# Regrouping the small products of the second attention layer, with a changed set-up, a changed step between the layers and both last norms on VectorE

## The reference

```
def layer0(x, emb, mask):                       # 16 heads of 32
    xn = layernorm(x) * norm_w + norm_b
    q, k, v = xn @ q_w + q_b, xn @ k_w + k_b, (xn @ v_w + v_b) * mask
    att = softmax over keys of (q k^T per head, masked)
    y = att @ v
    scale, shift = split(silu(emb) @ emb_w + emb_b)
    h = layernorm(y) * sb_w + sb_b;  h = h * (1 + scale) + shift
    return x + silu(h) @ out_w + out_b

def layer1(x, emb, mask):                       # 8 heads of 64
    xn = layernorm(x) * ln_w + ln_b
    q = softmax over a head's features of (xn @ Wq + bq)
    k = softmax over tokens of (xn @ Wk + bk, masked)
    v = (xn @ Wv + bv) * mask
    y = q @ (k^T v)                             # per head
    (the same norm of y, scale, shift, silu, output product, + x)
```

## Time and profile before

| | |
|---|---|
| median of 3 runs | 1053.91 us (1051.83 to 1054.78) |
| the profiled execution's own time | 1052.0 us |
| its span | 1048.6 us |
| TensorE busy | 1022.5 us, 98% of the span |
| VectorE, ScalarE, GpSimd busy | 772.7, 610.6, 588.1 us |
| mean granted TensorE clock | 0.997 of full |

### The profile page before, as it was taken

How to read it: one execution, slowest core, us unless ns; L and a number is a source line. 1 busy time by engine, 2 the same in 40 slices (tenths; PEclk the granted TensorE clock), 3 DMA queues, 4 the chain that set the end, 5 groups by cost and what they waited for, 6 DMA issues and landing times. The chain is left out here.

```text
span 1048.6 us, 26047 instructions
## 1 busy us (share of the span) xinstructions
PE 1022.5 (98%) x8558; PEld 890.0 (85%) x8558; DVE 772.7 (74%) x1347; ACT 610.6 (58%) x2021; POOL 588.1 (56%) x871
## 2 busy tenths in 40 slices
PE   7899999999999999999997999999999999999997
PEld 6679888988889888898886888888888888888885
DVE  6656766677666766678679787878778877778886
ACT  6358676876768766776777454434434444443353
POOL 3455456555465456554577465666556555566632
PEclk9999999999999999999999999999999999999999
DMA  9752111211212111120113211222211112112101
GB/s 302 246 184 67 39 52 43 64 55 35 60 44 65 47 40 53 55 65 34 56 51 116 81 63 50 67 67 65 65 65 56 39 55 65 55 55 65 45 31 50
DMA packets 46117, 73.72 MB, mean 70 GB/s; under 512 B 8274, under 2 KB 14546, under 8 KB 46068
## 3 DMA queue, kind: packets, MB, share of 16 engines
q1 hardware_dynamic: 46066, 73.11, 21.8%
q10 hardware_dynamic: 2, 0.00, 0.0%
HBM read 56.28 MB, written 16.81 MB: 70 GB/s over the span
## 5 line engine op out<-in xcount | busy, mean ns | idle before, releaser
L683 ACT ACTIVATE prob<-prob,neg_max 128x128 f32<-128x128 f32 x512 | 198.6, 395 | 77.7 <-DVE neg_max L983 77.7
L483 POOL TENSOR_SCALAR stat<-stat 128x1 f32<-128x1 f32 x128 | 34.7, 271 | 321.7 <-DVE stat L945 295.3
L1363 PE MATMUL bank<-xt_hi,w_hi 128*128 128x256 f32 x752 | 213.8, 284 | 0.0
L1364 PE MATMUL bank<-xt_lo,w_hi 128*128 128x256 f32 x752 | 209.4, 279 | 0.0
L1365 PE MATMUL bank<-xt_hi,w_lo 128*128 128x256 f32 x752 | 209.4, 278 | 0.0
L1363 PE MATMUL bank<-w_hi,xt_hi 128*128 128x512 f32 x384 | 157.6, 410 | 0.0
L1365 PE MATMUL bank<-w_hi,xt_lo 128*128 128x512 f32 x384 | 151.2, 394 | 0.0
L1364 PE MATMUL bank<-w_lo,xt_hi 128*128 128x512 f32 x384 | 150.4, 392 | 0.0
L1364 PEld LDWEIGHTS bank<-xt_lo,w_hi 128*128 128x128 f32 x752 | 141.9, 189 | 1.3
L1363 PEld LDWEIGHTS bank<-xt_hi,w_hi 128*128 128x128 f32 x752 | 141.6, 188 | 1.5 <-DVE z_a L1027 0.2
L1365 PEld LDWEIGHTS bank<-xt_hi,w_lo 128*128 128x128 f32 x752 | 141.7, 188 | 0.0
(11 more groups left out here) (130 smaller groups left out, 2347.4 us busy)
## 6 DMA issues: line engine op xcount, KB each, us to landing
x_in<-in_x_dram SPq DMA_DIRECT2D x32, 256.0 KB, 2.7
x_res<-in_x_dram SPq DMA_DIRECT2D x32, 256.0 KB, 2.6
between_layers<-x_res SPq DMA_DIRECT2D x32, 256.0 KB, 2.0
x_in<-between_layers SPq DMA_DIRECT2D x32, 256.0 KB, 3.3
x_res<-between_layers SPq DMA_DIRECT2D x28, 256.0 KB, 2.6
out_dram<-x_res SPq DMA_DIRECT2D x28, 256.0 KB, 2.0
room<-in_L_cond_W_emb_dram SPq DMA_DIRECT2D x8, 512.0 KB, 6.6
prob<-in_L_cond_emb_w_dram SPq DMA_DIRECT2D x4, 512.0 KB, 11.2
```

What stands on the lines that cost most here:

```text
L483: pool.tensor_scalar(v[:, 8:9], v[:, 7:8], EPS, None, ALU.add).then_inc(s[a_in].sem, 1)
L683: last = act.activation(prob[:, b, i, :], prob[:, b, i, :], ACT.Exp, bias=neg_max[:, b, i:i + 1], accum_out=row_sum[:, b, h:h + 1])
L1363: pe.matmul(o, a_hi, b_hi, start=start, stop=False)
L1364: pe.matmul(o, a_hi, b_lo, start=False, stop=False)
```

## The change

Seven things change together. (1) TensorE's order in `step1` and the first part of `drain`: both `turn_k`, both `keys`, both `keys_values`, both outputs, both `query`, both `values` and both `turn_yn` now stand together, and PSUM banks are dealt anew. (2) In `step1`, the scale (`film1`), `tanh`, `silu`, high and low part of both sequences of pair `k` move from the end of their step to the beginning of the next, where that pair is `late`. (3) POOL's second `v_mask` stands before the two residuals. (4) In `step_mixed` POOL makes `norm2` before the residuals and `v_mask`. (5) At the start VectorE norms both first pairs, with POOL making only their factors, and one values product comes earlier on TensorE. (6) `keep_busy` adds seven products of `ident` with itself, whose result nobody reads, around the first `turn`s. (7) In `drain` both last norms end on VectorE.

```diff
-        SECOND = dict(X=(0, 1), K=(6, 7), V=(0, 6), Q=(2, 4), KT=(2, 4), QT=(3, 3), KV=(4, 4), Y=(5, 1), H=(3, 7), O=(5, 1))
+        SECOND = dict(X=(0, 1), K=(6, 0), V=(6, 0), Q=(2, 4), KT=(2, 4), QT=(5, 5), KV=(4, 2), Y=(5, 4), H=(3, 7), O=(1, 3))
-        DRAIN = SECOND | dict(V=(0, 3), Q=(2, 4), KT=(6, 7), QT=(2, 4), KV=(0, 3), Y=(6, 7), H=(0, 3), O=(5, 4))
+        DRAIN = SECOND | dict(V=(7, 6), Q=(2, 3), KT=(0, 4), QT=(2, 2), KV=(6, 7), Y=(0, 4), H=(6, 7), O=(5, 3))
...
-                for b in range(GROUP):
-                    rsqrt(b, 0, "aggr", "rstd_a", "rstd_b", "neg_mean", pair(0) + b, "xn_turned")
+                for n in (pair(0), pair(1)):
+                    for b in range(GROUP):
+                        rsqrt(b, 0, "aggr", "rstd_a", "rstd_b", "neg_mean", n + b, "xn_turned")
                 pool.wait_ge(row_out, 2)
-                for b in range(GROUP):
-                    norm1(0, pair(1), b)
...
             def step_mixed(i, n, f, k, late, slot):
                 norm1(1, n, 0)
-                residual(0, k, 0)
                 norm1(1, n, 1)
-                v_mask(f, slot, 0)
                 norm2(k, 0)
                 add_shift(k, 0)
+                residual(0, k, 0)
+                norm2(k, 1)
+                v_mask(f, slot, 0)
                 residual(0, k, 1)
-                norm2(k, 1)
                 v_mask(f, slot, 1)
...
                 norm2(k, 0)
                 v_mask(f, slot, 0)
                 norm2(k, 1)
+                v_mask(f, slot, 1)
                 if i == G:
                     pool.wait_ge(out_in, 16)
                 residual(1, k, 0)
                 residual(1, k, 1)
-                v_mask(f, slot, 1)
...
             def step1(i, n, f, k, late, slot):
+                if i != G:
+                    film1(late + (-1), 0)
+                    tanh(late + (-1), 0)
                 kt_out(k, 0)
+                kt_out(k, 1)
                 qt_out(k, 0)
-                kt_out(k, 1)
                 q_exps(k, 1 - slot, 1)
+                if i != G:
+                    s_high(late + (-1), 0)
+                    film1(late + (-1), 1)
+                    tanh(late + (-1), 1)
                 s_high(late + (-1), 1)
                 qt_out(k, 1)
                 k_exps(f, slot, 0)
...
                 if i == G:
                     high_part(1, WO)
                     act.wait_ge(film_dve, 6)
-                film1(k, 0)
-                tanh(k, 0)
                 q_exps(f, slot, 0)
-                s_high(k, 0)
-                film1(k, 1)
                 xt_high(n, 1 - slot, 0, SECOND)
                 xt_high(n, 1 - slot, 1, SECOND)
-                tanh(k, 1)
...
-            def norm2_end(k, b):
+            def norm2_end(k, b, at):
...
-                dve.tensor_scalar(yn[:, b, :], y_s[:], v[:, 10:11], v[:, 9:10], ALU.add, ALU.mult
+                dve.tensor_scalar(yn[:, b, :], at[:], v[:, 10:11], v[:, 9:10], ALU.add, ALU.mult
                                   ).then_inc(s["yn_full"].sem, 1)
...
-                    first_norm(b)
+                    first_norm(f, b)
...
+                for b in range(GROUP):
+                    first_norm(pair(1), b)
...
                 s_low_part(late + (-1), 1)
+                stats1(n, 0)
                 softmax(k, 1, (0,))
-                stats1(n, 0)
                 stats1(n, 1)
...
             def step1(i, n, f, k, late, slot):
+                q_sums(k, 1 - slot, 0)
+                if i != G:
+                    silu(late + (-1), 0)
+                stats1(n, 0)
+                if i != G:
+                    s_low_part(late + (-1), 0)
+                stats1(n, 1)
+                q_sums(k, 1 - slot, 1)
+                k_masked(f, slot, 0)
+                if i != G:
+                    silu(late + (-1), 1)
+                k_highest(f, slot, 0)
+                k_masked(f, slot, 1)
+                s_low_part(late + (-1), 1)
                 if i == G:
-                    s_low_part(late + (-1), 1)
                     dve.wait_ge(zeroed, 1)
-                else:
+                kv_out(k, 1 - slot, 0)
+                kv_out(k, 1 - slot, 1)
+                k_highest(f, slot, 1)
+                if i != G:
                     output(SECOND, late + (-1), 0)
-                stats1(n, 0)
-                q_sums(k, 1 - slot, 0)
-                q_sums(k, 1 - slot, 1)
-                kv_out(k, 1 - slot, 0)
-                k_soft(f, slot, 0)
-                stats1(n, 1)
                 output(LAST_OUT if i == G else SECOND, late + (-1), 1)
-                k_soft(f, slot, 1)
                 y_norm(1, k, 1 - slot, 0)
-                kv_out(k, 1 - slot, 1)
+                k_inverse(f, slot)
                 v_add(1, SECOND, f, slot, 0)
                 y_norm(1, k, 1 - slot, 1)
-                k_inverse(f, slot)
+                v_add(1, SECOND, f, slot, 1)
                 if i == G:
                     low_part(1, WO)
                 q_add(SECOND, f, 0)
                 q_soft(f, slot, 0)
-                silu(k, 0)
-                v_add(1, SECOND, f, slot, 1)
-                s_low_part(k, 0)
                 q_add(SECOND, f, 1)
                 xt_low(n, 1 - slot, 0, SECOND)
                 xt_low(n, 1 - slot, 1, SECOND)
                 q_soft(f, slot, 1)
-                silu(k, 1)
-                s_low_part(k, 1)
...
                 y_norm(1, f, 1, 0, DRAIN)
+                y_norm(1, f, 1, 1, DRAIN, z_a)
+                norm2_end(f, 0, y_s)
                 s_low_part(k, 1)
-                norm2_end(f, 0)
-                y_norm(1, f, 1, 1, DRAIN, z_a)
-                output(LATE, k + (-GROUP), 1)
+                norm2_end(f, 1, z_a)
+                output(SECOND, k + (-GROUP), 1)
...
+            def keep_busy(n):
+
+                for _ in range(n):
+                    pe.matmul(bank[FIRST["Q"][1]][:, 0:P], ident[:], ident[:], start=True, stop=True)
...
                 for b in range(GROUP):
+                    keep_busy((4, 1)[b])
                     turn(f, b, BEGIN)
+                keep_busy(2)
                 first_queries(f)
...
+                need(0, WV)
+                values(0, BEGIN, f, 0, 0)
                 claim(2, times(cond_dve, 2))
                 pe.wait_ge(cond_dve, 1)
                 for k in range(KE):
                     last = pe.transpose(bank[2][:, k * B:(k + 1) * B], silu_rows[:, k * P:(k + 1) * P], ident[0:B, 0:B])
                 last.then_inc(cond_pe, 1)
-                need(0, WV)
-                values(0, BEGIN, f, 0, 0)
                 values(0, BEGIN, f, 0, 1)
...
                 need(1, WK)
-                keys(1, f, slot, 0)
-                keys(1, f, slot, 1)
+                keys(1, f, slot, 0, MIXED)
+                keys(1, f, slot, 1, MIXED)
...
             def step1(i, n, f, k, late, slot):
                 turn_k(k, 1 - slot, 0)
+                turn_k(k, 1 - slot, 1)
                 turn_q(k, 1 - slot, 0)
-                turn_k(k, 1 - slot, 1)
-                if i == G + 1:
-                    need(1, WO)
-                if i != G:
-                    output(1, SECOND, late + (-1), 0)
                 keys(1, f, slot, 0)
+                keys(1, f, slot, 1)
                 turn_q(k, 1 - slot, 1)
                 keys_values(k, 1 - slot, 0)
+                keys_values(k, 1 - slot, 1)
                 if i == G:
                     output(0, LAST_OUT, late + (-1), 1)
                 else:
+                    if i == G + 1:
+                        need(1, WO)
+                    output(1, SECOND, late + (-1), 0)
                     output(1, SECOND, late + (-1), 1)
-                keys(1, f, slot, 1)
                 query(k, 0)
-                keys_values(k, 1 - slot, 1)
+                query(k, 1)
                 values(1, SECOND, f, slot, 0)
-                query(k, 1)
+                values(1, SECOND, f, slot, 1)
                 queries1(SECOND, f, slot, 0)
-                turn_yn(1, k, 0)
-                values(1, SECOND, f, slot, 1)
                 queries1(SECOND, f, slot, 1)
-                turn_yn(1, k, 1)
                 turn(n, 0, SECOND)
                 turn(n, 1, SECOND)
+                turn_yn(1, k, 0)
+                turn_yn(1, k, 1)
```

More of the change, by code:

```diff
@@ L846, in step1 @@
                     act.wait_ge(film_dve, 6)
-                film1(k, 0)
-                tanh(k, 0)
                 q_exps(f, slot, 0)
-                s_high(k, 0)
-                film1(k, 1)
                 xt_high(n, 1 - slot, 0, SECOND)
                 xt_high(n, 1 - slot, 1, SECOND)
-                tanh(k, 1)
             def drain(k, f):
+                film1(k + (-GROUP), 0)
+                tanh(k + (-GROUP), 0)
                 kt_out(k, 0)
+                kt_out(k, 1)
                 qt_out(k, 0)
-                kt_out(k, 1)
                 q_exps(k, 0, 1)
+                s_high(k + (-GROUP), 0)
+                film1(k + (-GROUP), 1)
+                tanh(k + (-GROUP), 1)
```

(49 more changed lines are left out.)

27 lines of the change are left out of this document (12 added, 15 removed).

## The result

The changed kernel takes 1054.97 us (median of 22 runs, 1052.05 to 1057.59), before takes 1053.29 (22 runs, 1049.23 to 1055.26): ratio 1.0021, interval 1.0012 to 1.0030. The interval leaves out 1, so this is a small loss and not nothing. I had forecast 1047.6 and 6.3 us won; by the ratio 2.2 were lost (the medians differ by 1.7). The time lies just inside the upper end of my range, 1055, and on the other side of no change. The profiled execution of the changed kernel is its slowest, 1057.59, with a span of 1055.7.

What follows compares the result with a forecast made beforehand. TensorE, at 98% of the span, was taken as the bound. Steps −2.8, step_mixed −3.4, start −0.5 and drain +0.4 sum to −6.3 from the median 1053.91, giving 1047.6 us; range 1043 to 1055.

Steps and rivals of the forecast that it cites:

- The saving of regrouping, 0.35 a step: TensorE's small products in fewer stretches: 0.35 us saved a step, 0.25 to 0.45, −4.9 over 14 steps.
- 12.7: 0.3 early. I take 0.05 a step lost: Second output product in each step: its s_lo ready at 12.7 us, 0.3 early; 0.05 a step lost, 0 to 0.9.
- rival D: Steps: second s_lo late, both silu at 1.78 beside norm1; TensorE waits 0.8 a step, 1056.7 us in all; chance 0.12.
- I take 0.1 a step lost here: Keys in each step: they may wait for xt_lo behind 28 transposes; 0.1 us a step lost, 0 to 0.5.
- C: Rival: keys wait 0.3 to 0.4 us for xt_lo in every step, eating the 0.35; 1051.1 us; chance 0.20.
- step_mixed, −3.4: Between layers: yn earlier −4.0, clock stays −2.2, s_lo waits 2.0 here and next step, step 17 −1.2; −6 to −1.
- The start, −0.5: Start: earlier rows end a turn wait, mostly waited for again at the condition weights; −0.5 us, −2 to +0.5.
- The drain, +0.4: Drain: last yn made ahead of s_lo, regrouped first half saves 0.35 but meets new waits; +0.4 us, −1 to +1.5.
- E: Rival: transposes let the clock fall, 28 at half pace, 3.05 us longer a step, 1097 us; chance 0.02.

Runs made afterwards that it cites:

- the kernel of all three orders: Changed kernel with second late sequence's silu and low part earlier, residuals ahead of second norm2, step 16's late low part behind first q_sums: 1044.26 us, ratio 0.9930.
- x4_resid: Changed kernel with POOL's two residuals of a step moved ahead of the second norm2: ratio 0.9966 to before.
- the second profile: The changed kernel run once more, unchanged, for its trace: ratio 1.0025 to before.
- x11_norms_only: Kernel of before with only the last norm's end moved to VectorE and the drain order that goes with it: ratio 0.9995.

## Why the prediction was wrong

Taking the stretches of the changed kernel's two profiles against the one of before, the changed kernel gains nothing in step_mixed and 16 together, 0.9 in step 17, loses 2.8 in steps 18 to 29 and 1.0 in the drain, and gains about 0.7 at the start: +2.2, the measured difference. That it fits to the tenth is luck, as the start's term is not known to 1 us. My forecast by the same stretches was −2.4 in steps 18 to 29, −3.8 in step_mixed, 16 and 17, −0.5 and +0.4: of the 8.5 us that it was off, 5.2 are in steps 18 to 29, 2.9 in the steps before them and 0.6 in the drain, and the start was 0.2 better.

*The saving of regrouping, 0.35 a step: right.* 29.07 − 28.72 = 0.35 in the kernel of all three orders, where nothing waits in these steps.

*"12.7: 0.3 early. I take 0.05 a step lost": this is the step that failed.* Measured 29.28 − 28.72 = 0.56 a step, where I had 0.15 for both waits together. Nearly all of it is the second output product's wait for `s_lo`: from the first output product's start to the second's are 3.53 us in one step and 3.16 in the next, where the kernel of all three orders has 2.86, 0.49 a step where I had 0.05. So it happened at the place of rival D, milder than its 0.8, but not by D's cause: D had both `silu` at 1.78, and they took 0.69 and 1.30. What I had mis-sized is the time that the chain spends in VectorE's queue. My sum has `k_masked` and `stats1` in it, but it names no `q_sums` and nothing that makes the queue late from the step's start. The second `silu` started 718.77 − 717.36 = 1.4 after its `tanh` was done, behind `q_sums` and `k_masked`: that queue has hardly a gap, so what one operation loses, all behind it lose. The operation that lost most is `q_soft`'s first subtraction. I took 1.02 for it from the earlier trace rows; it takes 1.58 to 1.70 here, since it is held until the residuals end (with the second sequence's the mean is 1.17). So the second `s_lo` is done at 13.3 and 13.7 (721.37 + 0.67 − 708.37). `x4_resid` shows the subtraction's share: with the residuals elsewhere it is done at 12.9 and 13.2, and 0.42 a step are back. It alternates because at the loop's turn, every second step, VectorE's queue loses 0.4 us more (`silu` starts 5.50 behind the step's beginning at 713.87, and 5.11 behind it in the next).

*"I take 0.1 a step lost here", for the keys: about right.* They start 3.11 and 3.19 behind the step's beginning where the kernel of all three orders has 2.97. Its first output product starts no earlier, though (10.32 behind it, against 10.29 and 10.35), so C's wait is there and costs little. The 0.07 that is left of the 0.56 falls behind the outputs, and its cause is open.

This step alone does not make the sign: 14 × 0.41 = 5.7 would have left −0.6 of my −6.3. The loss needs the next part as well.

*step_mixed, −3.4: right in the place, wrong in the sum.* `yn` was 1.03 late (forecast 1), the clock stayed (−2.2 came), `s_lo` 1.65 (2.0) and 2.41 in step 16 (2.0; 2.20 in the second profile). What I missed is that the clock could fall behind the new wait as it had behind the old: the 12 products at 602.78 take 4.42 where twelve at the full level take 2.84, 1.6 us. Another 0.6 was a longer wait for `y_t` in step_mixed (0.94, before 0.30). With step 17's −0.9, this part gave −0.9.

*The start, −0.5: right as a mean,* −0.7 from a mean of 106.2 (eight profiles with the new start, one of them without the fillers) and 107.0 (five with the old one). But each group scatters over 4 us and more, 104.3 to 109.8, so its sign is not shown.

*The drain, +0.4:* +1.0. The norms gave −0.8; so the regrouping of its first half costs about 1.8, where I had a saving of 0.35 and the waits of a step. I did not take that apart by a run. The first profile lists waits of 0.81 (for `spare`, ahead of 1031.85), 0.96, 1.05 and 0.46 there, and that of `x11_norms_only` 0.45, 1.05 and 0.45, so 1.3 of it is waiting; in the second profile the one for `spare` is smaller, so it varies.

*E* did not happen: the transposes went at the full level's pace.

## What to carry to other kernels

Before an order is changed so that the bound engine reads what a helper writes at another time, write down when each of its inputs is ready and when it is wanted; a margin of 0.1 or 0.3 us at the end of a queue that has hardly a gap is none. When a queue is full, the place of an operation in it is the lever: three moves of existing instructions, none of them on TensorE, turned +0.2% into −0.7%. And the same contention was free in one order and cost 0.4 us a step in the other, so it can only be priced together with what waits behind it.
